# Experts of a two-layer graph, attention and mixture network: down products by half of their contraction, first gate bank by bank, eighth expert tile by tile

## Chip, core and metric

One core of a Trainium2 chip runs the whole program in one launch. The metric is the device time in microseconds (us), from the first to the last work of the core. The kernel before has a median of 3207.25 us over 3 runs (3206.21 to 3208.53).

## What is computed

`x` holds 1250 rows of 1024 float32 values. Two layers follow each other. Each adds a graph convolution and a linear attention to `x`, and then a mixture of experts. The change touches the experts alone:

```python
def _L0_ffn_ref(...):            # layer 0: 8 experts, top 2, at most 391 tokens each
    xe = x[tok_idx]              # gather the tokens of each expert
    h = silu(einsum('ech,ehi->eci', xe, gate_w)) * einsum('ech,ehi->eci', xe, up_w)   # i = 512
    ye = einsum('eci,eih->ech', h, down_w) * top_g[..., None]
    out = zeros_like(x).at[tok_idx.reshape(-1)].add(ye.reshape(-1, H))

def _L1_ffn_ref(...):            # layer 1: 8 experts, top 2, no capacity, hidden = 256
    hidden = silu(h1) * h2       # h1, h2: two halves of x @ w12
    expert_out = einsum('bteh,edh->bted', hidden, w3)
    y = sum(total_probs[..., None] * expert_out)      # over the two chosen experts
```

## The kernel before, in words

All large products run on TensorE as three float32r products: both operands are split in a high part (a cast by ScalarE) and a rest (a subtraction by VectorE), and `three` (its products are L489, L490, L491) adds high x high, high x rest and rest x high into one PSUM bank.

**Weights.** SyncE loads each unit of weights (1 MB) into `WS`, two places. ScalarE casts it in two halves into `WH` (L1322) and VectorE makes the rest (L1726); both do so one unit ahead, in `next_unit`, at fixed places of their own order. TensorE's `unit` waits on `wl_done` for the split unit. A `WH` place is written again when the products of the unit two before have ended (`u.end`).

**Work of the experts** (`experts(layer)` on TensorE, ScalarE and VectorE). Layer 0 has 8 blocks, one an expert, of 4 tiles of 98 tokens, hidden width 512. Layer 1 has up to 17 blocks of 2 tiles of 128 tokens, hidden width 256; a block belongs to one expert, and 15 blocks run with these inputs. GpSimd gathers the tokens of a block from `xn_d` (L1253) up to three blocks ahead. Then, per block:

- *Turns.* `turn_bank` transposes one 128-wide slice of the block's tokens into a bank of `PA` (L639, 4 transposes in layer 0 and 2 in layer 1). `PA` is a ring of two banks: ScalarE casts the bank into `xeT` (L1454), VectorE subtracts (L1907) and so frees it. There are 8 banks to a block. Those of the next block are turned behind the gate and up products of this one (`ffn_turns`); those of block 0 come first.
- *Gate and up.* `project` multiplies one unit of weights by the turned tokens: two banks of `PS` (gate) or `PV` (up), 24 products each. ScalarE applies Silu (L1476), VectorE multiplies (L1935), ScalarE casts the product into `hT` (L1485) and VectorE makes its rest (L1937, `hl_done`). Layer 0 has two units each of gate and up, layer 1 one each. In layer 0 the first gate of block b + 1 goes ahead of the down products of block b.
- *Down.* `down` multiplies `hT` by the down weights, one piece of 512 columns after the other, the pieces alternating between `PV` (emptied and scaled by VectorE, L1952) and `PS` (by ScalarE, L1500). In layer 0 the down weights are two units, one for each half of the columns, and the order is by half and then by tile. In layer 1 they are one unit, and the order is by tile and then by half. It begins behind one wait for all hidden values of the block:

```python
def down(b, full):
    pe.wait_ge(hl_done, hidden_base + mt * (b + 1))
```

- *Scatter.* GpSimd adds a finished tile (both halves) to `x2_d` or `out` by an indirect DMA (L1270). After layer 0, ScalarE reads `x2_d` back when all scatters have landed (L120, L121), and the second layer starts from there.

`PV` and `PS` are rings of three banks; `Bank.take` waits until the bank used three takes ago is emptied. In layer 0 an expert whose last tile has no token skips its products there but for one (`full`, L682).

Of the kernel before, what the change touches and what calls it, by code (L numbers as in the profile page):

```python
# [27 lines left out]
P = 128  # L28
T = 1250
D = 1024  # L30
# [3 lines left out]
KD = D // P  # L34
HALF = 512
# [4 lines left out]
E = 8  # L40
# [7 lines left out]
UNIT = 2048  # L48
# [82 lines left out]
def build(nc, A, out):  # L131
    ctx = ExitStack()
    with ctx:
# [319 lines left out]
        def _(pe):  # L453
# [172 lines left out]
            def experts(layer):  # L626
# [37 lines left out]

                def first_gate(b, full):
                    pe.wait_ge(t_free, gather_end[layer, b][1])
                    project(b, 0, 0, full)

                def down(b, full):
                    pe.wait_ge(hl_done, hidden_base + mt * (b + 1))  # L670
                    dcols = UNIT // mt
                    for nd in range(D // dcols):
                        u = unit("split")
                        w = [h.rearrange("p (k n) -> p k n", k=mt) for h in unit_parts(u)]
                        for t in range(tiles):
                            for n0 in range(0, dcols, HALF):
                                j = len(y_at)
                                ring = (v, s)[j % 2]
                                bank = ring.take(pe)
                                for k in range(mt if t < full else 1):  # L680
                                    if t >= full:
                                        mm = pe.matmul(bank[0:r, :], hT[:, 0, 0, 0:r], w[0][:, 0, n0:n0 + HALF],  # L682
                                                       start=True, stop=True)
                                        continue
                                    mm = three(bank[0:r, :], [hT[:, a, k, t * r:(t + 1) * r] for a in range(2)],
                                               [h[:, k, n0:n0 + HALF] for h in w], k == 0, k == mt - 1)
                                mm.then_inc(ring.full, 1)
                                y_at[j] = ring.n
                        u.end = (ring.full, ring.n)
# [7 lines left out]
                for k in range(KD):  # L697
                    turn_bank(0, k)
# [481 lines left out]
        def _(pool):  # L1180
# [56 lines left out]
            for layer in range(2):  # L1237
# [21 lines left out]
                def scatter(b):  # L1259

                    for t in range(tiles):
                        n = y_number(layer, b, t)
                        for half in range(2):
                            j = (0 if layer == 0 else E * 8) + b * npiece
                            j += half * tiles + t if layer == 0 else 2 * t + half
# [42 lines left out]
        def _(act):  # L1308
# [135 lines left out]
            def experts(layer):  # L1444
# [43 lines left out]
                def results(b):  # L1488
                    npiece = tiles * D // HALF
                    for p in range(npiece):  # L1490
# [220 lines left out]
        def _(ve):  # L1711
# [490 lines left out]
            n = 0  # L2202
# [334 lines left out]
```

## Time and profile before

| | |
|---|---|
| median of 3 runs | 3207.25 us |
| profiled execution, its own time | 3205.25 us |
| its span (first to last instruction) | 3203.5 us |
| TensorE, VectorE, ScalarE, GpSimd busy | 94%, 63%, 40%, 14% |
| granted TensorE clock over the span | 0.970 |
| experts of layer 0 (first turn to last product) | 1107.7 to 1561.0 us |
| experts of layer 1 (first turn to last product) | 2881.0 to 3191.4 us |

A row of the timeline gives start, duration, engine, line, operation, output <- input, count, and in square brackets the time that the engine stood idle before it and what released it. A row of the waits gives the total, the times and the longest. PE is TensorE, DVE is VectorE, ACT is ScalarE, POOL is GpSimd. A granted clock of 1.00 is 2.4 GHz, the lower level is 1.2 GHz; a mean of 0.70 over a stretch says that 0.60 of it ran at the lower level.

### The profile page before, as it was taken

What the parts mean: (1) busy time and instruction counts of PE and PEld (TensorE: products, weight loads), DVE (VectorE), ACT (ScalarE), POOL (GpSimd) and SP (SyncE); (2) the same over time, 40 slices, a digit from 0 to 9 for tenths busy, and PEclk for the clock granted to TensorE, in tenths of its full rate; (3) what the DMA queues carried; (4) which work ended last, traced back from release to release, by engine and by line L of the source; (5) the groups of instructions that cost most, each with busy time, mean ns of one, the idle gap of its engine ahead of it and who ended that gap; (6) DMA issues with size and microseconds to landing.
All of it is one profiled execution on the core that took longest, in us unless ns stands there. A gap on an engine that the chain in (4) does not pass through costs nothing.

```text
span 3203.5 us, 52951 instructions
## 1 busy us (share of the span) xinstructions
PE 2997.8 (94%) x22168; PEld 2749.1 (86%) x22168; DVE 2019.6 (63%) x3533; ACT 1266.0 (40%) x2173; POOL 454.2 (14%) x328
## 2 busy tenths in 40 slices
PE   6999999999999699999699999999999999979997
PEld 6998898379986598898599998899999999968887
DVE  7986477977886744444466665676355653656665
ACT  4463055444421034433354434444134521425554
POOL 1034443443000111211100000000000000002222
PEclk9999999999999799999899999999999999989999
DMA  8322112123044256654721000363322333248997
GB/s 276 104 59 44 1 17 58 1 55 82 1 115 138 48 159 180 180 155 134 194 90 36 31 29 29 105 158 89 95 82 67 101 80 105 92 134 233 263 266 211
DMA packets 261917, 344.39 MB, mean 108 GB/s; under 512 B 40706, under 2 KB 223016, under 8 KB 259988
## 3 DMA queue, kind: packets, MB, share of 16 engines
q1 hardware_dynamic: 169511, 211.56, 22.0%
q0 software_dynamic: 43312, 77.14, 12.2%
q10 hardware_dynamic: 48829, 51.86, 5.5%
q8 instruction: 202, 3.31, 0.4%
q14 instruction: 63, 0.52, 0.1%
HBM read 264.10 MB, written 76.40 MB: 106 GB/s over the span
## 4 chain that ended last, share of the span: by engine, by line
PE 85%; DVE 8%; issue 2%; ACT 2%; DMA 1%; SPq 0%; ACTq 0%; POOL 0%; DVEq 0%; POOLq 0%
PE PV L489 18%; PE PV L491 17%; PE PV L490 17%; PE PV L602 5%; PE PS L489 3%; PE PS L491 3%; PE PS L490 3%; PE PV L872 3%; PE PA L639 1%; PE PV L778 1%; PE PA L793 1%; PE PS L793 1%; PE PV L818 1%; DVE b L2037 1%; PE PA L833 1%
## 5 line engine op out<-in xcount | busy, mean ns | idle before, releaser
L489 PE MATMUL PV<-WH,b_split 128*125 128x256 f32 (+2 forms) x3708 | 1078.7, 291 | 53.7 <-DVE b_split L1737 34.0
L490 PE MATMUL PV<-WH,b_split 128*125 128x256 f32 (+2 forms) x3708 | 1065.7, 287 | 0.0
L491 PE MATMUL PV<-WH,b_split 128*125 128x256 f32 (+2 forms) x3708 | 1065.3, 287 | 0.3 <-issue 0.3
L1737 DVE TENSOR_TENSOR b_split<-b,b_split 128x500 fp32r<-128x500 f32 x1040 | 687.4, 676 | 397.6 <-ACT b_split L1332 379.6
L1332 ACT CAST b_split<-b 128x500 fp32r<-128x500 f32 x1040 | 626.5, 612 | 747.9 <-PE PV L491 723.9
L489 PEld LDWEIGHTS PV<-WH,b_split 128*125 128x125 f32 (+2 forms) x3708 | 690.8, 186 | 76.5 <-issue 31.1
L490 PEld LDWEIGHTS PV<-WH,b_split 128*125 128x125 f32 (+2 forms) x3708 | 693.5, 187 | 9.9
L491 PEld LDWEIGHTS PV<-WH,b_split 128*125 128x125 f32 (+2 forms) x3708 | 690.7, 186 | 12.0 <-issue 0.7
L1726 DVE TENSOR_TENSOR WH<-WS,WH 128x1024 fp32r<-128x1024 f32 x292 | 344.3, 1220 | 116.2 <-ACT WH L1322 115.0
L1322 ACT CAST WH<-WS 128x1024 fp32r<-128x1024 f32 x292 | 291.6, 1050 | 155.2 <-PE PV L602 141.8
L489 PE MATMUL PV<-b_split,WH 128*128 128x250 f32 (+3 forms) x1136 | 334.5, 294 | 0.5 <-issue 0.5
L490 PE MATMUL PV<-b_split,WH 128*128 128x250 f32 (+3 forms) x1136 | 329.8, 290 | 0.0
L491 PE MATMUL PV<-b_split,WH 128*128 128x250 f32 (+3 forms) x1136 | 329.0, 290 | 0.0
L1229 POOL DMA_INDIRECT at_d<-ecnt,eidx x168 | 273.1, 1625 | 389.1 <-DMA at_d<-ecnt,eidx 357.1
L1253 POOL DMA_INDIRECT b<-xn_d,tidx x66 | 66.0, 1000 | 1637.8 <-issue 1312.8
L489 PEld LDWEIGHTS PV<-b_split,WH 128*128 128x128 f32 x1136 | 215.2, 189 | 1.7 <-issue 1.3
L490 PEld LDWEIGHTS PV<-b_split,WH 128*128 128x128 f32 x1136 | 215.4, 190 | 0.2
L491 PEld LDWEIGHTS PV<-b_split,WH 128*128 128x128 f32 x1136 | 215.2, 189 | 0.0
L602 PE MATMUL PV<-WH,b_split 125*128 125x250 f32 x1600 | 197.0, 286 | 9.1 <-DVE b_split L1842 7.2
L602 PEld LDWEIGHTS PV<-WH,b_split 125*128 125x128 f32 x1600 | 193.6, 193 | 12.5 <-issue 7.6
L489 PE MATMUL PS<-b_split,WH 128*128 128x256 f32 (+2 forms) x496 | 156.5, 316 | 5.1 <-issue 3.0
L1907 DVE TENSOR_TENSOR b_split<-PA,b_split 128x256 fp32r<-128x256 f32 (+1 forms) x192 | 83.6, 465 | 114.5 <-ACT b_split L1454 114.1
(290 smaller groups left out, 3567.5 us busy)
## 6 DMA issues: line engine op xcount, KB each, us to landing
WS<-in_L_ffn_w SPq DMA_DIRECT2D x46, 1024.0 KB
WH<-at_d SPq DMA_DIRECT2D x15, 1093.8 KB
WS<-in_L_ffn_gate_w SPq DMA_DIRECT2D x16, 1024.0 KB
WS<-in_L_ffn_up_w SPq DMA_DIRECT2D x16, 1024.0 KB
WS<-in_L_ffn_down_w SPq DMA_DIRECT2D x16, 1024.0 KB
b<-key_d POOLq DMA_DIRECT2D x4, 2560.0 KB, 9.3
WS<-in_L_mix_Wv SPq DMA_DIRECT2D x8, 1024.0 KB
WS<-in_L_mix_Wk SPq DMA_DIRECT2D x8, 1024.0 KB
```

Of the source, the lines that this page charges most:

```text
L489: pe.matmul(o, a[0], b[0], start=start, stop=False, **kw)
L490: pe.matmul(o, a[0], b[1], start=False, stop=False, **kw)
L491: return pe.matmul(o, a[1], b[0], start=False, stop=stop, **kw)
L602: mm = pe.matmul(bank[:, 0:AC], part[:, j, f * P:(f + 1) * P].bitcast(dt), at[:, j, :], start=(j + a == 0), stop=(j + a == NT))
L872: mm = pe.matmul(bank[0:R, :], at[:, j, t * R:(t + 1) * R], part[:, j, half * HALF:(half + 1) * HALF].bitcast(dt), start=(j + a == 0), sto ...
L1229: pool.indirect_dma_start(out=at_d, out_offset=bass.IndirectOffsetOnAxis(ap=eidx[:, g:g + 1], axis=0), in_=ecnt[:, g:g + 1], in_offset=Non ...
L1253: pool.indirect_dma_start(out=ffn_xe(layer, b)[0:r, t, :], out_offset=None, in_=xn_d, in_offset=bass.IndirectOffsetOnAxis(ap=tidx[0:r, c:c ...
L1322: act.copy(WH[:, u.place % 2, a:a + UNIT // 2], WS[:, u.stage % 2, a:a + UNIT // 2])\
L1332: act.copy(hi, src).then_inc(xh_done, 1)
L1726: ve.tensor_tensor(WH[:, u.place % 2, UNIT + a:UNIT + a + UNIT // 2], WS[:, u.stage % 2, a:a + UNIT // 2], WH[:, u.place % 2, a:a + UNIT / ...
L1737: ve.tensor_tensor(lo, src, hi.bitcast(F32), ALU.subtract).then_inc(xl_done, 1)
L1907: ve.tensor_tensor(xeT[:, 1, k, :], bank, xeT[:, 0, k, :].bitcast(F32), ALU.subtract).then_inc(t_free, 1)
```

## The change

Four things change.

1. *Layer 1, down* (`down_rows`). The four pieces of a block are opened in four banks at once. The products of the first half of the contraction (k = 0) go through all four, behind a wait for the first hidden half; then those of the second half, behind a wait for the second.
2. *First gate of block 0, both layers* (`turned_gate`). Before, all 8 banks of tokens were turned, and then the gate unit's two banks were computed one after the other, with turns of block 1 behind each. Now the weights are waited for first, two banks are turned, and then the six products of slice k (three for each of two open gate banks) alternate with the turn of slice k + 2. The turns of block 1 follow behind the gate.
3. *Layer 0, eighth expert* (`by_tile`). Both down units are opened first, and the order is by tile and then by half. ScalarE's and VectorE's `results` follow: the unit behind the down weights is split at the end of the pieces.
4. *Layer 0, the other experts*. The first piece of down waits for each quarter of the hidden values by itself; the order of the products stays.

```diff
+                def turned_gate(full):
+                    xeT = ffn_xeT(layer, 0)
+                    wid, turned = full * r, tr.n
+                    u = unit("split")
...
+                    for m in range(2):
+                        banks.append(s.take(pe))
+                        gate_at[layer, m] = s.n
+                        turn_bank(0, m)
+                    for k in range(KD):
+                        pe.wait_ge(t_free, turned + k + 1)
+                        for m in range(2):
+                            mm = three(banks[m][:, 0:wid], [h[:, k, m * P:(m + 1) * P] for h in w],
+                                       [xeT[:, a, k, 0:wid] for a in range(2)], k == 0, k == KD - 1)
+                            if k == KD - 1:
+                                mm.then_inc(s_full, 1)
+                        if k + 2 < KD:
+                            turn_bank(0, k + 2)
+                    u.end = (s_full, s.n)
+                    for m in range(2):
+                        for k in ffn_turns(layer, 0, 0, m):
+                            turn_bank(1, k)
...
+                def down_rows(b):
+                    u, w = down_unit()
+                    banks = []
+                    for k in range(mt):
+                        pe.wait_ge(hl_done, hidden_base + mt * b + k + 1)
+                        for n in range(2 * tiles):
+                            if k == 0:
+                                banks.append(down_bank())
+                            ring, bank = banks[n]
+                            t, n0 = n // 2, n % 2 * HALF
+                            mm = three(bank[0:r, :], [hT[:, a, k, t * r:(t + 1) * r] for a in range(2)],
+                                       [h[:, k, n0:n0 + HALF] for h in w], k == 0, k == mt - 1)
...
                 def down(b, full):
-                    pe.wait_ge(hl_done, hidden_base + mt * (b + 1))
...
+                    by_tile = b == blocks - 1
+                    opened = [down_unit(), down_unit()] if by_tile else []
+                    order = [(nd, t) for t in range(tiles) for nd in range(2)] if by_tile else \
+                            [(nd, t) for nd in range(2) for t in range(tiles)]
...
+                            if n == 0:
+                                pe.wait_ge(hl_done, hidden_base + mt * b + k + 1)
...
-                for k in range(KD):
-                    turn_bank(0, k)
...
-                        if p % (UNIT // mt // HALF * tiles) == 0:
+                        if p == 0 or (p == tiles and not by_tile):
                             next_unit()
...
+                    if layer == 0 and by_tile:
+                        next_unit()
```

How TensorE's order moves, at three places. Rows give line, operation, output <- input and shape, and the semaphores that are waited for.

Layer 1, down of one block, before (behind the last two turned banks of the next block, up to the next gate):

```order
L639 MATMUL PA<-ident,b 128x128 [waits t_free]
L489 MATMUL PV<-WH,b_split 128x512 [waits v_free,wl_done,hl_done]
L490 MATMUL PV<-WH,b_split 128x512
L491 MATMUL PV<-WH,b_split 128x512
...
L489 MATMUL PS<-WH,b_split 128x512 [waits s_free]
...
L489 MATMUL PV<-WH,b_split 128x512 [waits v_free]
...
L489 MATMUL PS<-b_split,WH 128x256 [waits s_free,wl_done,t_free]
```

and now:

```order
L639 MATMUL PA<-ident,b 128x128 [waits t_free]
L489 MATMUL PV<-WH,b_split 128x512 [waits v_free,hl_done,wl_done]
L490 MATMUL PV<-WH,b_split 128x512
L491 MATMUL PV<-WH,b_split 128x512
L489 MATMUL PS<-WH,b_split 128x512 [waits s_free]
...
L489 MATMUL PV<-WH,b_split 128x512 [waits hl_done]
L490 MATMUL PV<-WH,b_split 128x512
L491 MATMUL PV<-WH,b_split 128x512
L489 MATMUL PS<-WH,b_split 128x512
...
L489 MATMUL PS<-b_split,WH 128x256 [waits s_free,wl_done,t_free]
```

A bank had its six products in one piece; now it has three in the first pass and three in the second, and the wait on `hl_done` stands ahead of each pass.

Layer 1, first gate, now (before, all 16 transposes of block 0 stood ahead of the first product):

```order
L639 MATMUL PA<-ident,b 128x128 [waits xe_full0,t_free,s_free,wl_done]
L639 MATMUL PA<-ident,b 128x128 [waits t_free,s_free]
L489 MATMUL PS<-b_split,WH 128x256 [waits t_free]
L490 MATMUL PS<-b_split,WH 128x256
L491 MATMUL PS<-b_split,WH 128x256
...
L639 MATMUL PA<-ident,b 128x128 [waits t_free]
L489 MATMUL PS<-b_split,WH 128x256 [waits t_free]
...
L639 MATMUL PA<-ident,b 128x128 [waits t_free,xe_full1]
L639 MATMUL PA<-ident,b 128x128 [waits t_free]
L489 MATMUL PV<-b_split,WH 128x256 [waits v_free,wl_done]
```

The wait for the gate's weights moved ahead of the first transpose, and the four banks of block 1 are turned in one run between the gate and up. ScalarE's order is the same before and now: eight casts of turned banks, then

```order
L1322 CAST WH<-WS 128x1024 [waits ws_full1,v_full,v_free,acc_init1]
L1322 CAST WH<-WS 128x1024
L1476 ACT_TABLE_LOAD [waits s_full]
L1476 ACTIVATE RB<-PS 128x256 [waits hl_done]
L1454 CAST b_split<-PA 128x256 [waits t_full] x2
```

so the cast that frees the third bank of block 1 stays behind the first Silu.

Layer 0, eighth expert, first pieces of down, before:

```order
L489 MATMUL PV<-WH,b_split 98x512 [waits v_free,wl_done,hl_done]
...
L489 MATMUL PS<-WH,b_split 98x512 [waits s_free]
...
L489 MATMUL PV<-WH,b_split 98x512 [waits v_free]
...
L682 MATMUL PS<-WH,b_split 98x512 [waits s_free]
L489 MATMUL PV<-WH,b_split 98x512 [waits v_free,wl_done]
```

and now:

```order
L489 MATMUL PV<-WH,b_split 98x512 [waits v_free,hl_done,wl_done]
L490 MATMUL PV<-WH,b_split 98x512
L491 MATMUL PV<-WH,b_split 98x512
L489 MATMUL PV<-WH,b_split 98x512 [waits hl_done]
...
L489 MATMUL PS<-WH,b_split 98x512 [waits s_free]
...
L742 MATMUL PV<-WH,b_split 98x512 [waits v_free]
L742 MATMUL PS<-WH,b_split 98x512 [waits s_free]
```

The second wait on `wl_done`, ahead of the fifth piece before, is part of the first product's now; the two products of the empty tile (L682, now L742) end the expert.

## Rows read from the trace of the kernel before

**Rows 1.** The page, busy time of TensorE, its share and its instructions.
```profile
PE 2997.8 (94%) x22168; PEld 2749.1 (86%) x22168; DVE 2019.6 (63%) x3533; ACT 1266.0 (40%) x2173; POOL 454.2 (14%) x328
```
**Rows 2.** Waits of TensorE from 2880 us to the end: total, times, longest.
```profile
PE PV L489 <- DVE b_split L1937: 14.6, 15, 1.0
```
**Rows 3.** Timeline, TensorE and VectorE in two blocks of layer 1.
```profile
2897.92 0.60 PE L639 MATMUL PA<-ident,b 128*128 128x128 f32 x4
2898.28 0.36 PE L489 MATMUL PV<-b_split,WH 128*128 128x256 f32 x1
...
3102.91 0.43 DVE L1937 TENSOR_TENSOR b_split<-RB,b_split 128x256 fp32r<-128x256 f32 x1 [0.47 <-ACT b_split L1485]
3104.22 0.60 PE L639 MATMUL PA<-ident,b 128*128 128x128 f32 x4
3105.31 0.43 DVE L1937 TENSOR_TENSOR b_split<-RB,b_split 128x256 fp32r<-128x256 f32 x1 [0.47 <-ACT b_split L1485]
3105.79 0.50 PE L489 MATMUL PV<-WH,b_split 128*128 128x512 f32 x1 [0.97 <-DVE b_split L1937]
...
3111.37 0.28 PE L489 MATMUL PS<-b_split,WH 128*128 128x256 f32 x1
```
**Rows 4.** Windows (last three: granted clock, DMA share, GB/s), and ScalarE's wait for weights.
```profile
2926.00:2966.00 40.00, 37.98 (x272) 35.57 (x272) 25.77 (x42) 21.86 (x42) 10.38 (x9) 1.00 0.95 262
...
ACT WH L1322 <- DMA WS<-in_L_ffn_w: 0.2, 1, 0.2
```
**Rows 5.** Timeline of GpSimd, the last two scatters of layer 1.
```profile
3190.21 1.55 POOL L1270 DMA_INDIRECT out_x<-b,sidx  x1 [15.62 <-DVE b L1952]
3192.94 1.56 POOL L1270 DMA_INDIRECT out_x<-b,sidx  x1 [1.18 <-ACT b L1500]
```
**Rows 6.** Timeline of layer 1's first gate, and the window around it.
```profile
2880.96 1.09 PE L639 MATMUL PA<-ident,b 128*128 128x128 f32 x4
2881.30 2.35 DVE L1726 TENSOR_TENSOR WH<-WS,WH 128x1024 fp32r<-128x1024 f32 x2
2889.29 0.58 PE L489 MATMUL PS<-b_split,WH 128*128 128x256 f32 x1 [0.92 <-DVE b_split L1907]
2894.85 1.28 ACT L1476 ACT_TABLE_LOAD   x1 [4.18 <-PE PS L491]
2896.14 0.38 ACT L1476 ACTIVATE RB<-PS 128x256 f32<-128x256 f32 x1
...
2880.00:2926.00 46.00, 40.25 (x270) 36.89 (x269) 26.99 (x46) 22.46 (x45) 8.11 (x7) 0.84 0.71 205
```
**Rows 7.** Timeline of layer 0's first gate, and the window around it.
```profile
1107.71 1.57 PE L639 MATMUL PA<-ident,b 98*128 98x98 f32 x8 [3.64 <-DMA b<-xn_d,tidx]
1116.73 0.69 PE L489 MATMUL PS<-b_split,WH 128*128 128x392 f32 x1 [1.17 <-DVE b_split L1907]
1117.98 1.28 ACT L1476 ACT_TABLE_LOAD   x1
1127.72 0.42 PE L489 MATMUL PV<-b_split,WH 128*128 128x392 f32 x1
...
1107.00:1128.00 21.00, 17.55 (x94) 16.16 (x95) 7.92 (x12) 8.68 (x15) 4.39 (x4) 0.70 0.71 175
```
**Rows 8.** Timeline around the down products of layer 0's eighth expert.
```profile
1543.62 0.47 PE L489 MATMUL PV<-WH,b_split 128*98 128x512 f32 x1 [1.81 <-DVE b_split L1937]
1543.94 2.36 DVE L1726 TENSOR_TENSOR WH<-WS,WH 128x1024 fp32r<-128x1024 f32 x2 [0.38 <-ACT WH L1322]
...
1564.26 1.53 POOL L1270 DMA_INDIRECT x_d<-b,sidx  x1 [0.30 <-issue]
1571.90 0.32 ACTq L120 DMA_DIRECT2D b<-x_d  x1
```
**Rows 9.** A wait of TensorE near 2468 us, and the window around it.
```profile
2467.96 1.09 PE L498 MATMUL PS<-ident,b 125*128 125x125 f32 x4 [4.17 <-ACT b L1353]
...
2465.00:2475.00 10.00, 4.85 (x22) 4.50 (x23) 2.45 (x4) 4.27 (x8) 0.00 (x0) 0.66 0.33 102
```

## Prediction before the run

> **What bounds the kernel now.** I began with the page's busy times and the granted clock. TensorE is busy for 94% of the span [rows 1], so a saving counts only where TensorE waits or runs at its lower clock, and every new wait of TensorE counts in full. The change touches the two expert stages, so I asked there who keeps TensorE waiting. In the second layer's stage there is one steady wait: 15 times 0.97 us until VectorE's L1937, the low half of the hidden values [rows 2]. Then I read one block in order of time [rows 3]. Its last two turned banks (L639) start at 3104.22, and the first down product starts at 3105.79. Where nothing is waited for, the product after such a turn starts 0.36 us behind it (2897.92 to 2898.28). So a block loses 1.57 - 0.36 = 1.21 us: the wait and the restart behind it. The row of whole blocks shows the second resource: granted clock 1.00, but the DMA engines busy at a share of 0.95 with two blocks in 40 us [rows 4].
>
> **The change, part by part.**
>
> *A. Down products by half of their contraction (layer 1, 15 blocks).* The same 24 products of 512 columns. The first twelve need only the first hidden half, done at 2.4 us before the second: L1937 ends at 3103.34 and at 3105.73 [rows 3]. The first is ready before the turns end. Twelve products at 0.23 us (the 24 of a block run from 3105.79 to the next gate at 3111.37) take 2.8 us from 3104.58, so the second half is wanted at about 3107.3, 1.6 us after it is there. All four banks are opened at once; each ring of three has the bank free that is asked for, since the gate's and up's first banks were read before that hidden half existed. A block loses its 1.21 us of waiting: 15 x 1.21 = **-18.2 us**. What is late next: the split of the next gate's weights, and the loads. The lower bound of the gain comes from [rows 4]: if a share of 0.95 in 20.0 us can only become 1.00, a block can't fall under 19.0 us, which leaves 15 x 0.95 = 14.3 us.
>
> *B. The last block's tail.* The two pieces of a tile now end in the last quarter of the pass, 0.7 us apart. The piece that frees the first scatter ends 1.4 us before the last product instead of 2.8. Now the scatters are issued 2.73 us apart (3190.21 and 3192.94) [rows 5], and 1.55 + 0.30 us is the closest that they can follow. The second goes from 1.7 to about 2.2 us behind the last product, and lands behind a closer neighbour: +0.5 to +1.3, I take **+1.0 us**. In the other blocks no one waits for a scatter.
>
> *C. First gate of layer 1.* Its weights are asked for ahead of the turns now. VectorE splits them until 2881.30 + 2.35 = 2883.65, while TensorE turned from 2880.96 [rows 6]. From there the first bank is ready after some 1.6 us (two banks turn in 1.09, then a cast and a rest of about 0.4 each, and the passing on), and the first product starts near 2885.3 instead of 2889.29. Then eight rounds of six products and a turn: a product follows the last by about 0.22 us there (256 columns; the 512 of [rows 3] take 0.23 at the full clock, and twice that at half), so a round is 6 x 0.22 + 0.55 = 1.9 us at the lower clock and, bound by the way of a bank, 1.1 at the full one. A granted clock of 0.84 over the 46 us from 2880 means 14.7 us at the lower clock, so it rose at 2894.7, 5.4 us behind the first dense product [rows 6]. If it rises as long behind the new first product, near 2891, the gate ends near 2896; if at 2894.7 again, near 2897.4. But both banks end together. ScalarE has in its queue, after the eighth cast, two weight casts (2.0 us), then the table load that waits for the gate (1.28, and the Silu starts 1.29 after it) [rows 6], then Silu, then the cast of the next block's first bank. TensorE has to turn four banks of that block through a ring of two, so it stands at the third until ScalarE and VectorE have come so far: up begins near 2899.8 to 2901.6 instead of 2898.28. I take the middle, **+2.5 us**; bounds 0 (the table load hidden) and +5 (a further stretch at the lower clock). The Trainium skill (ScalarE: Activation LUTs, What ACT_TABLE_LOAD costs) adds a drain of 1.38 us to every table switch. The row shows none of it, so it is not in the sum; by the page this term would be +3.9.
>
> *D. First gate of layer 0.* The same with four transposes to a bank. First product near 1109.8 (one bank's way, 0.8 for the turn, 0.5 and 0.6 for cast and rest and the passing on, from 1107.71) instead of 1116.73 [rows 7]. A product of 392 columns is 392/256 of one above, 0.34 us at the lower clock and 0.18 at the full one, so a round is 2.8 or 1.5 us. The clock rose at 1119.6 (0.70 granted over the 21 us from 1107), 2.9 us behind the first dense product. The new stream starts 7 us earlier but has turns in it; I let the clock rise near 1116, and the gate ends near 1123.9; the last bank's cast, the two weight casts, the table load (hidden before, at 1117.98), Silu, one cast and one rest put the third turn near 1127.3 and up near 1127.8, against 1127.72. **0 us**; bounds -1.7 (clock up at about 1113) and +1.6 (at 1119.6).
>
> *E. Eighth expert tile by tile.* Both down units are opened before the first product. The second's split ends at 1543.94 + 2.36 = 1546.30, and down starts now at 1543.62, behind the first unit alone [rows 8]: **+2.7 us**. TensorE then stands for 4.5 us instead of 1.81. A wait of 4.17 us at 2468 is followed by a granted clock of 0.66 over 10 us, thus 6.8 us at the lower clock [rows 9]; so much would cost the stream 3.4 us, none would cost nothing. I take **+2.5**, since this wait, the nearest in length, lost its clock. In return the first two tiles' scatters leave early, and the last one (issued 1564.26, landed by 1571.90) has one close before it instead of three [rows 8]: 0 to -2, I take **-1.5**. Sum of E: +3.7, bounds +0.7 and +6.1. x2 is read back only behind the last scatter, so this is all on the path. The later split of V's first weights lies in that gap and costs nothing while the gap is over 20 us.
>
> Other blocks of layer 0: only the waits of the first piece become four, all long fulfilled behind the next gate: 0. SP and GpSimd keep their order of loads; the third gather waits for the eighth turned bank, some 6 us later, and is wanted a block later: 0.
>
> Sum: -18.2 + 1.0 + 2.5 + 0 + 3.7 = **-11.0 us**. The profiled execution took 3205.25 (span 3203.5): 3194.3. The median of the runs lies 2.0 above it: **3196.3 us**.
>
> **Rivals.**
> 1. *The ends come cheap*: the clock rises early in both gates and holds over the wait of E. C 1, D -1.7, E +1.2: net -16.7, 3190.6 us. For it: a wait of 1.81 there left the clock at full. Against: 4.17 did not. Chance 0.12.
> 2. *DMA becomes the bound of layer 1.* For it: share 0.95 already, and the two scatters of a block now leave together and sit on the load of the next down weights. Against: the loads have some slack, as ScalarE waits 0.2 us in all for one [rows 4]. Block 19.0 us: -14.3 + 7.2 = -7.1, 3200.2 us; half of its spread is within 0.2%. Chance 0.25. The Trainium skill (DMA: Bandwidth & Descriptors, Issuing engines are not separate DMA queues) says that what SP and GpSimd issue runs on the same 16 engines and interleaves, so moving bytes between queues would give nothing back.
> 3. *Slower: late loads take all of the gain.* Place: the split of the next gate's or down's weights in each of the 15 blocks. If scatter pairs hold a load back by as much as the 1.21 us and its slack, a block stays at 19.97 us and only the costs remain: +7.2, 3214.5 us. It decides against the change once a block gains under 0.5 us. Against: the bytes of a block are the same. Chance 0.05.
> 4. *Banks in rotation cost the clock.* Down goes from bank to bank every three products instead of six; were TensorE at half clock in them, 24 x 0.19 x 15 = 68 us more, about 3265 us. Against: it changes banks every six now at a granted 1.00 [rows 4]. Chance 0.02. It is the Trainium skill's second failure mode (TensorE: Matmul & The Clock Gate, A second HAM failure mode: psum-queue depth-cycling): cycling through banks can make the clock swing. The trace of before does not agree for six products; three it does not show.
> 5. *The ends come dear*: C 4, D 1.6, E 6: -5.6, 3201.7 us. Chance 0.06.
>
> **How the numbers follow.** The forecast (A in full, ends between their bounds) has 0.50. 0.2% is 6.4 us, about what a measurement of this kernel can tell from no change. Under 3200.8 lie the forecast, rival 1, half of rival 2 and little else: 0.75. Slower by over 6.4 lie rivals 3 and 4 in the main: 0.06. The rest is 0.19. The range runs from rival 1 to just past rivals 2 and 5, 3190.5 to 3202.5.
>
> **What would show it.** Right: the wait for L1937 before down gone in layer 1; blocks 18.8 us apart instead of 19.97; down in the eighth expert starting near 1546 and at the lower clock; a new wait of TensorE before the third turned bank behind each first gate, with ScalarE's table load in it. Wrong: blocks at 19.5 or more with ScalarE or VectorE waiting for WS; the clock under 1.00 inside layer 1's blocks; up beginning earlier than 1126 or 2898; the x2 read back at 1571.9 or before.

## The result, and the profile after

The changed kernel takes 3211.39 us (median of 20 runs, 3204.70 to 3218.37) against 3207.11 us of the kernel before (20 runs on the same chips, 3203.62 to 3209.50). The ratio is 1.0014, 95% interval 1.0008 to 1.0020. So it is 4.3 us slower (0.14%); the forecast was 3196.3 with a range of 3190.5 to 3202.5. The profiled execution took 3208.42 us, 3 us under the median; its span is 3206.7 us against 3203.5.

The program can be cut at places that both traces show, and the 3.2 us between the spans laid out over the stretches. (After the eighth expert TensorE starts again at 1582.88 before and at 1594.63 after; the other cuts are in the rows.)

| stretch | before | after | difference |
|---|---|---|---|
| up to the first turn of layer 0 | 1107.71 | 1105.37 | -2.3 (the same code, a matter of chance) |
| first turn to first up product | 20.0 | 25.8 | +5.8 |
| from there to the wait before the eighth down | 414.1 | 418.9 | +4.8 |
| from there to TensorE's restart on x2, read back | 41.1 | 44.6 | +3.5 |
| from there to the split of layer 1's first gate weights | 1298.4 | 1303.8 | +5.3 |
| that split to the first up product of layer 1 | 17.0 | 17.4 | +0.4 |
| from there to the end | 305.2 | 290.9 | -14.3 |

Two of the lines (+4.8 and +5.3) lie where the change moves next to nothing, and the first gate of layer 0, forecast at nothing, is the dearest place of all. Of the +4.8 us, 1.8 are a lower clock right behind the first up product (VectorE reads the first up bank 7.6 us later behind the first turn than before); the other 3 come at later branches, up to 1330 us.

**First gate of layer 0.** Timeline of TensorE, ScalarE and VectorE, in order of time [rows 7]:

```profile
1105.37 1.54 PE L639 MATMUL PA<-ident,b 98*128 98x98 f32 x8 [2.85 <-DMA b<-xn_d,tidx]
1107.43 0.70 PE L489 MATMUL PS<-b_split,WH 128*128 128x392 f32 x1 [0.52 <-DVE b_split L1966]
...
1119.65 2.36 DVE L1785 TENSOR_TENSOR WH<-WS,WH 128x1024 fp32r<-128x1024 f32 x2 [0.48 <-ACT WH L1378]
1120.40 0.84 PE L639 MATMUL PA<-ident,b 98*128 98x98 f32 x8
1120.49 1.28 ACT L1532 ACT_TABLE_LOAD   x1
1123.31 0.56 PE L639 MATMUL PA<-ident,b 98*128 98x98 f32 x4 [2.07 <-DVE b_split L1966]
1131.17 0.66 PE L489 MATMUL PV<-b_split,WH 128*128 128x392 f32 x1 [7.30 <-issue]
```

Up to 1123.31 it goes better than forecast: the gate begins 2.1 us behind the first turn, ends at about 1120.6, and the third turned bank waits as foreseen, with the table load in the wait. But then TensorE stands for 7.3 us, and the row says "issue": nothing that it needs is late. The up weights are split by 1122.01 (VectorE's row at 1119.65), the `PV` banks are free. The windows (last three columns: granted clock, DMA share, GB/s) show the clock that this costs. It fell while TensorE stood:

```profile
1107.00:1128.00 21.00, 14.31 (x84) 13.29 (x84) 10.66 (x15) 10.57 (x17) 4.39 (x4) 0.83 0.50 124
1128.00:1138.00 10.00, 6.83 (x30) 6.82 (x31) 0.43 (x1) 0.00 (x0) 0.00 (x0) 0.64 0.74 193
1123.90:1131.10 7.20, 0.00 (x0) 0.00 (x0) 2.93 (x3) 2.38 (x3) 0.29 (x1) 0.57 1.03 267
```

The page has a queue of its own for code (packets, MB, share), and the DMA view of the second stretch, 1124 to 1131.2 us, has one packet of it, when the engines are full with the next weights and gathers; from 1110.95 to 1124 that view has none. Narrower windows put the packet at 1128.15 to 1129.43, so it starts 4.3 us after TensorE has gone idle, and up begins 1.7 us behind its end:

```profile
q8 instruction: 202, 3.31, 0.4%
```

```profile
DMA  7896698999999999999999999796999998989999
...
q8 instruction: 1, 0.02, 1.1%
```

The last line, from 1128 to 1129.6 us alone:

```profile
q8 instruction: 1, 0.02, 5.0%
```

**Far behind, in layer 1's graph convolution**, TensorE stands once more for "issue", in the middle of a bank, and loses its clock. A code packet lands here too, from 2714.66 to 2715.59, but it starts at once, 0.1 us after TensorE has gone idle. Timeline and window:

```profile
2713.46 0.35 PE L489 MATMUL PV<-WH,b_split 128*125 128x256 f32 x1 [1.66 <-issue]
...
2714.24 0.28 PE L489 MATMUL PV<-WH,b_split 128*125 128x256 f32 x1
2717.07 0.57 PE L490 MATMUL PV<-WH,b_split 128*125 128x256 f32 x1 [2.55 <-issue]
```

```profile
2711.00:2724.00 13.00, 8.79 (x52) 8.41 (x52) 1.96 (x4) 1.83 (x3) 0.00 (x0) 0.74 0.28 81
```

The kernel before has a first wait there too (1.7 us at 2701.59), but not the second.

**Eighth expert** [rows 8]. Both splits are waited for, as forecast, but the clock is lower over less than forecast: 0.91 granted over 20 us is 3.6 us at the lower level. Down takes 18.9 us where it took 17.4 (window of before, then rows and window of now):

```profile
1543.00:1563.00 20.00, 17.38 (x74) 11.98 (x74) 8.20 (x9) 6.50 (x8) 3.65 (x3) 1.00 0.39 100
```

```profile
1552.17 2.36 DVE L1785 TENSOR_TENSOR WH<-WS,WH 128x1024 fp32r<-128x1024 f32 x2 [0.38 <-ACT WH L1378]
1554.63 0.44 PE L489 MATMUL PV<-WH,b_split 128*98 128x512 f32 x1 [4.59 <-DVE WH L1785]
```

```profile
1554.00:1574.00 20.00, 18.89 (x74) 12.91 (x74) 3.38 (x5) 2.22 (x4) 3.06 (x2) 0.91 0.44 98
```

**First gate of layer 1** [rows 6]:

```profile
2898.41 2.35 DVE L1785 TENSOR_TENSOR WH<-WS,WH 128x1024 fp32r<-128x1024 f32 x2
2900.81 1.12 PE L639 MATMUL PA<-ident,b 128*128 128x128 f32 x4 [2.55 <-DVE WH L1785]
2902.42 0.58 PE L489 MATMUL PS<-b_split,WH 128*128 128x256 f32 x1 [0.49 <-DVE b_split L1966]
...
2912.79 1.28 ACT L1532 ACT_TABLE_LOAD   x1
2915.25 0.77 PE L639 MATMUL PA<-ident,b 128*128 128x128 f32 x4 [2.43 <-DVE b_split L1966]
2915.77 0.36 PE L489 MATMUL PV<-b_split,WH 128*128 128x256 f32 x1
```

No branch follows here, and no idle time does: up begins 0.5 us behind the third turned bank.

**Blocks of layer 1** [rows 2 to 4]. The wait for the low half (now L1996) has no row left in TensorE's waits. A block in which nothing disturbs goes from gate to gate in 18.73 us:

```profile
3060.86 0.28 PE L489 MATMUL PS<-b_split,WH 128*128 128x256 f32 x1
...
3073.68 0.60 PE L639 MATMUL PA<-ident,b 128*128 128x128 f32 x4
3074.03 0.48 PE L489 MATMUL PV<-WH,b_split 128*128 128x512 f32 x1
```

But over 13 blocks (gates at 2927.96 and 3174.46) the mean is 18.96. ScalarE now waits for loads (waits from 2926 to 3190 us), 9.7 us where it was 0.2, at a DMA share of 0.96:

```profile
ACT WH L1378 <- DMA WS<-in_L_ffn_w: 9.7, 12, 1.6
```

```profile
2926.00:2966.00 40.00, 39.48 (x282) 36.92 (x281) 26.87 (x42) 22.50 (x41) 11.71 (x8) 1.00 0.96 275
```

The last two scatters stand as close as forecast, 1.85 us apart [rows 5], and the last product (3192.96) now lies 1.2 us further from the end than it did:

```profile
3193.99 1.55 POOL L1326 DMA_INDIRECT out_x<-b,sidx  x1 [14.93 <-DVE b L2012]
3195.84 1.56 POOL L1326 DMA_INDIRECT out_x<-b,sidx  x1 [0.31 <-issue]
```

### The profile page after: what moved, and what is told of

It is laid out like the page before. It is cut to its first block, busy times and chain, and to the rows that moved or that the text cites. A ratio compares the mean times of both kernels' runs of the same rounds, so it can differ in the third digit from the quotient of the medians.

```text
span 3206.7 us, 52952 instructions
## 1 busy us (share of the span) xinstructions
PE 2999.3 (94%) x22168; PEld 2751.1 (86%) x22168; DVE 2017.7 (63%) x3533; ACT 1267.2 (40%) x2173; POOL 465.1 (15%) x328
## 3 DMA queue, kind: packets, MB, share of 16 engines
q0 software_dynamic: 43312, 77.14, 11.9%
q8 instruction: 202, 3.31, 0.4%
## 4 chain that ended last, share of the span: by engine, by line
PE 85%; DVE 9%; issue 3%; ACT 2%; DMA 1%; ACTq 0%; POOL 0%; DVEq 0%; SPq 0%; POOLq 0%
PE PV L489 18%; PE PV L490 17%; PE PV L491 17%; PE PV L602 5%; PE PS L489 3%; PE PS L491 3%; PE PS L490 3%; PE PV L928 3%; PE PA L639 2%; DVE b L2099 1%; PE PV L834 1%; PE PA L849 1%; PE PS L849 1%; PE PV L874 1%; DVE b_split L1796 1%
```

## The experiments

Each kernel was timed in five rounds beside the kernel before, whose median was 3206.4 to 3206.9 in the four sets of runs. The last column is the ratio to it with its 95% interval. The intervals are some 3 to 4 us to either side, so a difference of two medians is good to a few us, and those of under 3 us say nothing. Differences to "the change" set its 20 runs against runs of another time. "Spare" are products of TensorE in a branch that is not taken.

| run | what it has | median us | ratio to before |
|---|---|---|---|
| e1_rows | down by contraction in layer 1 alone | 3191.84 | 0.9957 (0.9943 to 0.9970) |
| e4_rows_gate1 | e1 + new first gate of layer 1 | 3192.09 | 0.9964 (0.9950 to 0.9977) |
| e7_rows_gate0 | e1 + new first gate of layer 0 | 3205.99 | 0.9997 (0.9988 to 1.0006) |
| e3_old_gate0 | the change, old first gate in layer 0 | 3197.77 | 0.9975 (0.9966 to 0.9984) |
| e5_no_tile8 | the change, old order in expert 8 | 3205.22 | 1.0001 (0.9992 to 1.0010) |
| e11_joined | e7, one branch instead of two | 3203.47 | 0.9991 (0.9982 to 1.0000) |
| e15_gate0_plain | e7, no branch there, 102 spare | 3192.55 | 0.9958 (0.9944 to 0.9972) |
| e10_spare | e1 + 32 spare in the first gate | 3201.66 | 0.9982 (0.9973 to 0.9991) |
| e13_spare128 | e1 + 128 spare in the first gate | 3196.29 | 0.9966 (0.9955 to 0.9977) |
| e19_spare128_down | e1 + 128 spare in the first down | 3192.15 | 0.9952 (0.9939 to 0.9966) |
| e14_gate0_96 | e7 + 96 spare in the first down | 3201.22 | 0.9985 (0.9976 to 0.9994) |
| e20_aligned | the change + 96 spare there | 3205.96 | 0.9996 (0.9987 to 1.0005) |
| e18_before32 | before + 32 spare in the first gate | 3218.80 | 1.0036 (1.0022 to 1.0050) |
| e12_late_unit | e3, expert 8's second weights asked for later | 3192.24 | 0.9961 (0.9947 to 0.9974) |
| e16_all | the change with e12's and e15's edits | 3192.71 | 0.9960 (0.9946 to 0.9973) |
| e17_half_loads | e1, half of each load in layer 1 | 3188.19 | 0.9944 (0.9931 to 0.9958) |

**1. The change taken apart.** For layer 0's old gate, the eight turns stand ahead of the branch again and `first_gate` calls `turned_gate` in layer 1 alone (`and layer in (1,)`); for the old eighth expert, `by_tile = False` in layer 0 on every engine.

e1_rows: 

> Only the down products of the second layer go by half of their contraction; both first gates and the eighth expert are as before. Theory G (the time was lost at the first gate of the first layer and at the eighth expert, and the second layer's blocks gained in full): 17 to 18 us less than before, about 3190, blocks 18.8 us apart, the wait for the hidden rest gone. Rival L (loads or their order take the gain back in the second layer): at most 14 us less than before, blocks over 19.0 apart. Rival P (where in the program an instruction fetch falls changes with its length, and costs 5 us or more in places the change does not touch): under 14 us less, with blocks at 18.8 and a stall in the second graph layer's rows near 2714 as in the changed kernel.

e3_old_gate0: 

> The changed kernel, but the first gate of the first layer as before (turns first, then the gate). Theory G: the 7.3 us in which TensorE stood idle behind the third turned bank, and the half clock behind it, are gone: 8 to 10 us less than the changed kernel, about 3202 (7 to 9 less than before is possible if nothing else costs). Rival L or P: under 4 us less than the changed kernel, because what it loses lies elsewhere.

e5_no_tile8: 

> The changed kernel, but the eighth expert's down products in the old order, with its second weights asked for in the middle. Theory G: the wait before the eighth down falls from 4.6 us to 1.8 and its half clock goes, the read-back of x2 comes 0.8 later: 3.5 us less than the changed kernel. Rival (the early scatters are worth more than the wait): no change or up to 2 us more.

e7_rows_gate0: 

> Down products by half of their contraction in the second layer, and the new first gate in the first layer alone; the second layer's first gate and the eighth expert as before. Theory G: 8 to 10 us more than the kernel with the down products alone, about 3199, with TensorE idle for some 7 us between the third turned bank of the next expert and the first up product. Rival P: within 3 us of the kernel with the down products alone.

Theory L falls as a main cause: the down products alone give 14.6 us. The new first gate of layer 0 costs 14.2 us (e7 against e1) and 13.6 (change against e3), half as much again as theory G said. The tile order costs 6.2 (change against e5); the ratios, which set each kernel against the one before in its own set of runs, give 4.2. And the stall near 2710 is in the trace of every kernel with the new first gate of layer 0 (the change, e5, e7) and in none of the others (before, e1, e3): theory P holds as well as G, beside it. From e7, waits of TensorE from 2700 to 2760 us:

```profile
PE PV L490 <- issue: 2.7, 1, 2.7
```

**2. Is it the branch behind the wait?** What lies between the third turned bank and the first up product is the end of one branch on the token count (`sized`) and the start of the next. e11 puts gate and hidden columns of expert 0 under one; e15 under none (it drops the arm that expert 0 doesn't take, so it is a probe for these inputs and not a kernel for all):

```diff
-if layer == 1 or b == 0:
-    sized(b, lambda full: first_gate(b, full))
-sized(b, lambda full: hidden_columns(b, full))
+if layer == 0 and b == 0:
+    sized(b, lambda full: (first_gate(b, full), hidden_columns(b, full)))
...
```

```diff
...
+if layer == 0 and b == 0:
+    first_gate(b, tiles)
+    hidden_columns(b, tiles)
...
```

e11_joined: 

> The kernel with the down products and the new first gate of the first layer, but with the first gate and the rest of the hidden columns of expert 0 under one branch instead of two. Theory B (TensorE's 7 us of idle time behind the third turned bank is the fetching of code behind the branch, which starts only when the wait ahead of it is over): the idle time falls under 1 us, the half clock behind it goes too, 8 us less than with two branches, near 3198; the stall near 2710 may stay. Rival W (it waits for the up weights, a bank or the engines behind it): the 7 us stay, same time within 2 us, near 3206.

e15_gate0_plain: 

> The down products and the new first gate of the first layer, with no branch around expert 0's first gate and hidden columns (its tokens need all four tiles here), and 102 products that are never run so that the code behind lies as in the kernel with the down products alone. Theory B: no idle time of TensorE behind the third turned bank, and none ahead of the first turn; up begins 3 us earlier than with the old gate, near 1124: 2 to 4 us less than the kernel with the down products alone, near 3189. Rival (the idle time was not the branch): 3196 or more, and the 7 us stay.

In e11 the idle time behind the third turned bank is gone, as theory B said, and yet only 2.5 us are won. The idle time has moved to the one branch that is left, ahead of the first turn, where TensorE also has nothing in hand; there the code packet starts 7.7 us after TensorE has gone idle, and the turn follows 1.6 us behind its end:

```profile
1113.92 1.54 PE L639 MATMUL PA<-ident,b 98*128 98x98 f32 x8 [10.42 <-issue]
```

In e15, with no branch, there is none in either place. From its timeline and windows, the same places as above:

```profile
1128.52 0.56 PE L639 MATMUL PA<-ident,b 98*128 98x98 f32 x4 [2.07 <-DVE b_split L1975]
1128.86 0.42 PE L489 MATMUL PV<-b_split,WH 128*128 128x392 f32 x1
```

```profile
1128.00:1138.00 10.00, 9.48 (x58) 9.41 (x59) 5.47 (x8) 3.94 (x7) 1.09 (x2) 1.00 0.99 268
```

The time is e1's within what was measured (3192.55 against 3191.84): without a branch the new gate costs nothing. In the traces VectorE reads the first up bank 23.1 us behind the first turn in e15 and 24.0 in e16, where it is 25.0 in e1, so the new gate wins 1 to 2 us there; in the medians this does not show, and the expected 2 to 4 us did not come.

That these waits are fetches of code is read from the packets. The traces of before, the change and all 16 runs hold 73 "issue" waits of TensorE of over 1.3 us, and each ends 1.2 to 2.1 us behind the end of a code packet of 16384 bytes. In the 67 of 1.4 to 3.1 us the packet starts between 1.6 us before and 0.7 us after TensorE goes idle; in the long ones behind a wait, 4.2 to 4.8 us after it (7.7 in e11). What holds it back there is not shown: the DMA engines are full (share 1.03), but near 1272 us a packet starts at once at a share of 0.98.

**3. Is it where the code lies?** The 32 transposes of block 0 stood ahead of the branch once and now stand in both of its arms, so the program is 32 products of TensorE longer. The spare products put as many into an arm that expert 0 doesn't take, and change nothing that runs:

```diff
 bank = ring.take(pe)
+for _ in range(spare * (1 - m)):
+    pe.matmul(bank[:, 0:wid], w[0][:, 0, 0:P], xeT[:, 0, 0, 0:wid], start=True, stop=True)
```

e10_spare: 

> The kernel with the down products alone, plus 32 products of TensorE in the branch that expert 0 does not take, in its first gate: they are never run, but everything behind them lies 32 instructions later in the program, as in the kernels with the new first gate of the first layer. Theory P (the later stall of 2.7 us near 2710 and its half clock come from where the program's code now lies): that stall shows up here too, and the time is about 5 us over the kernel with the down products alone, near 3197. Rival N (the stall comes from what the new gate does at run time, its later schedule of loads): no stall there, and the same time within 2 us, near 3192.

e13_spare128: 

> The kernel with the down products alone plus 128 products in the branch that expert 0 does not take, where the run before had 32. The trace's fetches of code are packets of 16384 bytes, one in about 16 us where a product comes every 0.12 us, so some 128 products of TensorE to a packet. Theory P (what costs is how code lies against these packets): with a whole packet more, everything behind lies as without any, so the stall near 2710 is gone and the time is back at 3192 within 2 us. Rival (any added code costs, by its amount): 3202 or more.

e19_spare128_down: 

> The kernel with the down products alone plus 128 products that are never run, in expert 0's down products instead of its first gate. If the 4 us that 128 of them cost in the first gate are the longer jump ahead of it (TensorE stood 2.6 us between its turns and its first product), they go here: 3192. If any 128 cost as much: 3196.

e14_gate0_96: 

> The down products, and the new first gate of the first layer (32 products more in the program), plus 96 products that are never run, in expert 0's down products: 128 in all. Theory P: the stall near 2710 goes, 7 to 9 us less than without the 96, near 3197. Theory B: TensorE still stands 7 us behind the third turned bank, so it stays 4 to 6 us over the kernel with the down products alone.

e20_aligned: 

> The whole change plus 96 products that are never run in expert 0's down products, 128 with the 32 that the new first gate brings. The stall near 2710 goes and the one behind the third turned bank stays: about 5 us less than the change, 3206, as much as the kernel before.

e18_before32: 

> The kernel before, with the same 32 products that are never run in expert 0's first gate and nothing else. Theory P: the placement of code costs the kernel before as much as the one with the down products alone: 8 to 10 us more, near 3216, with the stall of 2.7 us near 2720. Rival (the cost came with the new order of the down products): within 2 us of before.

32 products that never run cost 9.8 us (e10), and 11.9 in the kernel before (e18), where nothing else was changed. With 128 it is 4.5 (e13), and the stall near 2710 is gone; in another place, behind work that TensorE has in hand, 128 cost nothing (e19, 3192.15). So 5.4 us of e10's 9.8 go when the 32 become 128, about what the stall near 2710 takes (5.0 in the traces, e10 against e1). The rest lies in the first layer's experts: from the first turn to the "issue" wait near 1320 us e10 takes 4.7 us longer than e1, and e18 5.4 longer than the kernel before. The expectation of e19 puts this on a longer jump into the gate. That is not shown: e10 begins its gate behind the same 1.18 us wait for VectorE as e1, and stands behind it, 1.06 us at the first up product (e18: 2.14) and 1.04 near 1233. Only e13 stands at the gate, where its 2.64 us are 1.5 more than e1's wait:

```profile
1116.05 0.67 PE L489 MATMUL PS<-b_split,WH 128*128 128x392 f32 x1 [2.64 <-issue]
```

The 96 spare products take 4.8 us from e7 (e14) and 5.4 from the change (e20). The wait behind the third turned bank stays in e14, and the later stall goes. With it go some 3 us at the branches between the first up bank and 1330 us, while e14 stands longer at the first up product (7.8 us against 7.1). Waits of TensorE in e14, from 1104 to 1140 us, and the only "issue" row from 2700 to 2760:

```profile
PE PV L489 <- issue: 7.8, 1, 7.8
```

```profile
PE PV L489 <- issue: 1.7, 1, 1.7
```

A detail shows best that the later stall hangs on an address. In the change, e5, e7, e10 and e18, all 32 products longer, TensorE stops behind the 7th product of that bank; in e11, which has one If and Else less, behind the 8th. Its timeline:

```profile
2709.04 0.35 PE L489 MATMUL PV<-WH,b_split 128*125 128x256 f32 x1 [1.52 <-issue]
...
2709.94 0.28 PE L490 MATMUL PV<-WH,b_split 128*125 128x256 f32 x1
2712.68 0.58 PE L491 MATMUL PV<-WH,b_split 128*125 128x256 f32 x1 [2.46 <-issue]
```

Just ahead of this bank ends a long branch on the number of edges. The reading that fits, argued and not tested by itself, is that TensorE runs out of code that it has fetched since the jump, before the next packet is there; with no shift the packet's border comes 32 products later (3.8 us at the 0.12 us between products there), and the packet is in time. That the unit is a packet of 16 KB fits with 128 being harmless and 32 not; other numbers were not tried.

**4. The eighth expert and layer 1's gate.**

```diff
-opened = [down_unit(), down_unit()] if by_tile else []
+opened = []
```

e12_late_unit: 

> The changed kernel with the old first gate in the first layer, and the eighth expert tile by tile, but asking for the second down weights behind the first piece instead of ahead of it. If the wait for both splits and the clock behind it are what the tile order costs: down starts 2.8 us earlier, waits some 1.6 us behind its first piece, and keeps the clock, so 1.5 to 3 us less than with both asked for first, near 3195.5. If the tile order costs by something else (the scatters or the read-back): no change.

e4_rows_gate1: 

> The kernel with the down products alone, plus the new first gate of the second layer, where no branch follows. From the changed kernel's trace: +0.4 us, 3192; the forecast on record said +2.5. A rival (code fetch exposed there too) would give +7 or more.

Asking for the second unit behind the first piece gives back 5.5 us (4.5 by the ratios), all that the tile order cost: e12 is as fast as e4, which has the old order. In e12's timeline the first piece covers the second split, and it starts before the last of the four hidden rests is done (1542.00, not shown):

```profile
1541.52 0.45 PE L489 MATMUL PV<-WH,b_split 128*98 128x512 f32 x1 [1.28 <-DVE RB L1997]
1542.38 2.36 DVE L1788 TENSOR_TENSOR WH<-WS,WH 128x1024 fp32r<-128x1024 f32 x2 [0.39 <-ACT WH L1381]
1544.80 0.47 PE L489 MATMUL PS<-WH,b_split 128*98 128x512 f32 x1 [0.29 <-DVE WH L1788]
```

The expectation was 1.5 to 3; it left out this early start, but 5.5 is not clear of 3 with these intervals. Layer 1's gate costs 0.25 us in the medians, which can't be told from nothing and fits the 0.4 of its trace.

**5. Why a block gains 1.0 and not 1.21 us.** In layer 1 the products of e17 use old numbers for half of their rows, so it tells time alone (`lead` is given for the loads of layer 1's experts):

```diff
+if lead:
+    dst, src = dst[:, :, 0:k // 2], src[:, :, 0:k // 2]
 sp.dma_start(dst, src).then_inc(ws_full[u.stage % 2], 16)
```

e17_half_loads: 

> The kernel with the down products alone; in the second layer every load of weights brings only half of its rows of each expert (its products then use old numbers for the other half, the instructions are the same). If late loads are what keeps the blocks at 18.97 us on average instead of 18.72: ScalarE's waits for WS in the second layer (10 us in 14 waits) go, all blocks stand at 18.72, 3 to 4 us less, near 3188. Rival (the clock or code fetching stretches the blocks): they stay at 18.7 to 19.5 in the same manner, and the time at 3192.

All of its blocks behind the second gate stand 18.70 to 18.71 us apart, ScalarE has no wait for `WS` there, and it is 3.65 us faster than e1. Window of e17 over the same blocks:

```profile
2926.00:3186.00 260.00, 248.80 (x1794) 235.03 (x1792) 170.92 (x268) 144.57 (x267) 79.66 (x54) 0.98 0.77 188
```

The wait for loads goes with the uneven blocks, so late loads are the cause: over this window the DMA share is 0.94 before, 0.95 in e1 and 0.77 here. In the full kernels single blocks take 19.0 to 20.2 us and the others 18.7.

**6. All advice together.**

e16_all: 

> The whole change with what the runs so far advise: no branch around expert 0's first gate and hidden columns, the eighth expert's second weights asked for behind its first piece, code behind aligned as before. 2 to 4 us less than the same without the new first gate of the first layer (3192.2), near 3189; 18 us less than the kernel before. If branches and code placement were not the cause: 3197 or more.

It beats the kernel before by 13.7 us, and e1 not at all. Five kernels (e1, e4, e12, e15, e19) and this one lie between 3191.84 and 3192.71, which these runs can't tell apart. The simplest is e1: the down products of layer 1 alone are the whole gain.

## Why the prediction was wrong

- **A, down by contraction, -18.2:** the mechanism was right, the size 3 us off. The wait is gone and down follows the last turn by 0.35 us, but late loads stretch the blocks to 18.96 us: 15 x 1.01 = 15.2 us. Rival 2 (DMA becomes the bound, blocks of 19.0) had cause and size, though it comes as single late loads and not as a steady pace; the forecast should have been it. With B, e1 gave 14.6 us. The floor of 19.0 us was itself no floor: undisturbed blocks take 18.72.
- **B, the tail, +1.0:** the last product lies 13.3 us before the end, where it was 12.1: +1.2.
- **C, layer 1's first gate, +2.5:** +0.4 in the trace, +0.25 in e4. The wait with the table load came (2.43 us); but the clock rose 4.3 us behind the first product and not 5.4 (a granted 0.71 over the 46 us from 2880 is 26.7 us at the lower level, up to 2906.7), and the next block's first turns begin at 2912.22, 11.5 us behind the split, where 12.4 to 13.8 were charged. The 1.38 us drain that the prediction cites from the Trainium skill (ScalarE: Activation LUTs, What ACT_TABLE_LOAD costs) does not show here either: the activation starts 1.30 us behind the table load's start (2912.79, 2914.09), 0.02 behind its end, also where the weight casts end right ahead of it.
- **D, layer 0's first gate, 0 with bounds -1.7 to +1.6: the step that failed**, by 14 us. The sum followed TensorE's data (turns, casts, rests, table load) to the third turned bank near 1127.3, and put the first up product 0.5 us behind it, without asking what the sequencer does there. The old gate ended in products that were in hand while the branch was passed; the new one ends in a wait. Of the 14 us, 8 to 9 are that (e14 against e1 9.4, e20 against e3 8.2): 7.3 us idle, and the lower clock (0.64 granted in the ten us from 1128 is 7.2 us at the lower level, 3.2 of them still in the wait), which costs 1.8 us behind it. The other 5 (4.8 in e14, 5.4 in e20) come of 32 products more in the program: the stall near 2710 (5 us), and in the traces some 3 us more at the branches up to 1330 us, which e14 has lost but makes up for by its longer wait at up. The forecast counted what the change runs, and not how long it makes the code. "Other blocks of layer 0: 0" was right of what the change runs there.
- **E, tile by tile, +3.7:** the wait +2.8 (forecast +2.7), the clock +1.5 (+2.5), the scatters -0.8 (-1.5): +3.5 in the trace, about 6 in the medians (6.2 by e5, 5.7 by e3 against e4) and 4.2 and 3.5 in the ratios, with an interval of some 3 us around each. The mechanism was right; whether it is more than 3.5 stays open.

A row of the kernel before could have warned. Its waits of TensorE between 1126 and 1345 us hold two "issue" rows, of 3.0 and 2.2 us, in the part of the program that has a branch for every step of an expert:

```profile
PE PS L489 <- issue: 3.0, 1, 3.0
PE PS L491 <- issue: 2.2, 1, 2.2
```

The Trainium skill has the mechanism (Runtime: NRT & Kernel Launch, Instruction fetch mechanics): code comes in blocks of 16 KiB, fetched in sequence ahead of need, and a taken branch out of what is held fetches its target before going on. The packets of the code queue (202 for 3.31 MB) and the runs with spare products agree; here it was up to 3.1 us with work in hand, 7.1 to 7.8 behind a wait and 10.4 in e11, and the lower clock comes on top.

The sum by what was measured: -14.6 (A, B) + 0.3 (C) + 14 (D) + 6 (E) = +5.7 us, against +4.3; with E at 3.5 it is +3.2.

## What to carry to other kernels

Branches passed with work in hand cost 0 to 3.1 us here, one behind a wait 7.1 to 7.8 (with the DMA engines full): before moving a wait, look for the next branch behind it, and for "issue" rows of that engine near branches. When a change makes the program longer or shorter, run the old kernel with as much code that is never run, or the change with the difference filled up; ten microseconds in 3200 came from that alone here. And when two weights were asked for before the first product, the second one's wait was paid in full; asked for behind the first piece it cost nothing that shows.

## What was not expected of the hardware

- 32 products in an arm that is not taken made two kernels 9.8 and 11.9 us slower; 128 in another arm made no difference (0.3 us).
- Every "issue" wait of TensorE of over 1.3 us ended 1.2 to 2.1 us behind the end of a packet of code. Behind a branch that followed a wait it took 7.1 to 7.8 us (change, e5, e7, e14, e20), with the weights' and gathers' transfers on the same DMA engines, and in e11 TensorE stood for 10.4 us ahead of its first turn, where the other kernels stand 2.7 to 3.8 us for the gather.
- Going from bank to bank every three products in layer 1 left the granted clock at 1.00 over those blocks, as did every six.
